# GpSimd takes two products of the mixing stage, its bursts lose their clears, and the denominator is scanned first

## The reference, cut to what matters

```python
x = x + attn_a(layernorm(x), ...)
x = x + ffn(layernorm(x), ...)       # 8 experts, 2 for each token
x = x + attn_b(layernorm(x), ...)    # mixing
x = x + ffn(layernorm(x), ...)
# mixing, for each batch and feature, over the 1024 tokens:
#   numerator aa and denominator bb are carried, pp is the running maximum
q = maximum(pp, u + kt);  e1 = exp(pp - q);  e2 = exp(u + kt - q)
y = (e1 * aa + e2 * vt) / (e1 * bb + e2)
q2 = maximum(pp + w, kt); e1 = exp(pp + w - q2); e2 = exp(kt - q2)
aa, bb, pp = e1 * aa + e2 * vt, e1 * bb + e2, q2
out = (sigmoid(r) * y) @ Wo.T
```

## Time and profile before

| | us |
|---|---|
| median of 3 runs | 1177.89 (1176.38 to 1179.65) |
| profiled execution, its own time | 1185.97 |
| its span | 1184.1 |
| busy over the span: PE, DVE, ACT, POOL | 842.3, 705.8, 571.2, 731.5 |
| POOL: row DMAs of `scatter`, 256 | 300.3 busy, 1173 ns each |
| POOL: clears, 508 | 133.2 busy, 262 ns each |
| POOL: idle until `place_i` | 203.6 |

### The profile page before, as it was taken

The page is one execution under the profiler, slowest core; times in us unless marked ns, Lnnn a source line. Parts: engine busy times, 40 slices in busy tenths (PEclk is TensorE's granted clock), DMA queues, the critical chain, the costliest instruction groups (busy, mean ns, idle before and its releaser), DMA issues.

```text
span 1184.1 us, 19270 instructions
## 1 busy us (share of the span) xinstructions
PE 842.3 (71%) x4480; PEld 667.6 (56%) x4481; DVE 705.8 (60%) x2510; ACT 571.2 (48%) x1588; POOL 731.5 (62%) x1127
## 2 busy tenths in 40 slices
PE   3787867767429889898755667566721988988981
PEld 1565656646318778787722334333420877877871
DVE  5697867845524444444647888889750343655555
ACT  3776646642213233333768887988620333323320
POOL 3017876736745777777710378787784576766774
PEclk9779878866659999999977888778755999999996
DMA  6022232112255555556412232231233555777874
GB/s 182 19 59 86 89 87 76 53 36 70 79 129 166 148 155 155 157 155 196 129 54 71 85 98 80 76 95 45 60 104 79 153 153 179 230 216 227 241 211 138
DMA packets 160255, 142.69 MB, mean 121 GB/s; under 512 B 17817, under 2 KB 133154, under 8 KB 160070
## 3 DMA queue, kind: packets, MB, share of 16 engines
q1 hardware_dynamic: 121744, 70.98, 21.9%
q10 hardware_dynamic: 20854, 37.24, 10.3%
q0 software_dynamic: 17600, 33.87, 8.4%
HBM read 93.47 MB, written 50.37 MB: 121 GB/s over the span
## 4 chain that ended last, share of the span: by engine, by line
PE 43%; ACT 17%; DVE 11%; issue 11%; POOL 7%; another core or an unknown queue 6%; DMA 2%; ACTq 2%; DVEq 1%; SPq 0%; POOLq 0%
PE banks L1055 16%; PE banks L1075 6%; POOL queue_dram L567 5%; PE banks L927 4%; PE banks L953 4%; ACT qkv L737 2%; ACT hmix L636 2%; PE banks L960 2%; PE banks L1110 2%; ACT gated L746 2%; PE banks L1063 2%; PE banks L1111 2%; PE banks L981 1%; DVE gated L1403 1%
## 5 line engine op out<-in xcount | busy, mean ns | idle before, releaser
L580 POOL DMA_INDIRECT result_dram<-ytile,result_row x284 | 277.9, 979 | 165.4 <-remote 57.5
L567 POOL DMA_INDIRECT queue_dram<-hffn,place_i x256 | 300.3, 1173 | 60.4 <-issue 46.0
L1055 PE MATMUL banks<-xt,tile_up 128*128 128x256 f32 x1136 | 286.2, 397 | 35.8 <-DVE gated L1403 31.6
L746 ACT ACTIVATE gated<-banks,tile_bias 128x256 f32<-128x256 f32 x284 | 119.2, 473 | 302.7 <-PE banks L1055 130.5
L1055 PEld LDWEIGHTS banks<-xt,tile_up 128*128 128x128 f32 x1136 | 213.4, 198 | 69.2 <-issue 28.3
L1403 DVE SCALAR_TENSOR_TENSOR gated<-banks,tile_bias,gated 128x256 f32<-128x256 f32 x284 | 124.2, 480 | 170.9 <-ACT gated L746 104.5
L1075 PE MATMUL banks<-wdown_sb,gated 128*128 x1136 | 156.4, 281 | 17.4 <-DVE ytile L1411 9.1
L1075 PEld LDWEIGHTS banks<-wdown_sb,gated 128*128 128x128 f32 x1136 | 142.0, 195 | 22.1 <-issue 21.7
L542 POOL MEMSET spacer<- 128x176 f32 x508 | 133.2, 262 | 0.4
L557 POOL COPY hffn<-top_f 128x4 f32<-128x4 f32 x32 | 5.0, 190 | 203.6 <-DVE place_i L1301 203.6
L1411 DVE TENSOR_TENSOR ytile<-banks,down_bias_sb 128x256 f32<-128x256 f32 x142 | 59.5, 419 | 76.1 <-remote 41.4
(11 more groups left out here) (203 smaller groups left out, 1570.2 us busy)
## 6 DMA issues: line engine op xcount, KB each, us to landing
tile_up<-w_up ACTq DMA_DIRECT2D x142, 256.0 KB
xtile<-queue_dram SPq DMA_DIRECT2D x142, 130.0 KB
qkv<-result_dram SPq DMA_DIRECT2D x24, 512.0 KB
x_dram<-xres SPq DMA_DIRECT2D x32, 256.0 KB
result_dram<-ytile,result_row POOLq DMA_INDIRECT x284
xin<-x SPq DMA_DIRECT2D x16, 256.0 KB
xold<-x SPq DMA_DIRECT2D x16, 256.0 KB
queue_dram<-hffn,place_i POOLq DMA_INDIRECT x256
```

The source lines that it names most:

```text
L567: nc.gpsimd.indirect_dma_start(queue_dram, bass.IndirectOffsetOnAxis(ap=place_i[s][:, at:at + 1], axis=0), hffn[s][c][:, j, :], None).then ...
L580: nc.gpsimd.indirect_dma_start(result_dram, bass.IndirectOffsetOnAxis(ap=result_row[i % SLOTS][:, h:h + 1], axis=0), ytile[i % SLOTS][:, h ...
L746: last = nc.scalar.activation(gated[i % GSLOTS][:, h, :], ps_up[i % 2][:, h, :], ACT.Silu, bias=tile_bias[i % STEP][:, h:h + 1])
L1055: last = nc.tensor.matmul(ps_up[i % 2][:, h, :], tile_up[i % WSLOTS][:, h * P:(h + 1) * P], xt[i % 2][:], start=True, stop=True)
```

## The change

- The bursts of the mixing stage (scatters 9 to 16) are issued without clears.
- VectorE's product of the denominator, `expo` part 0 times `den` into `y_den`, goes to GpSimd: `denominators(row)`. For rows 3 to 8 it stands amid the burst, behind the tenth DMA (`AMID = 9`); for rows 1 and 2, which have no burst beside them, by itself. It waits for VectorE's scan (`den_scanned`) and ScalarE's `now_ex`; VectorE waits for it (`den_scaled`) before its addition to `y_den`.
- VectorE scans the denominator first, then makes `ev`, then the shifts, then the numerator's scan.
- `weigh` of first halves goes from ScalarE (eight instructions) to GpSimd (one, 128 x 1024, the gates broadcast), behind the burst. ScalarE waits for both halves before the next clamps.
- The semaphore `numbered` and its wait in `scatter` go; `bias_in`, `split_out` and `rows_in` of the setup become one, `bias_moved`.

```diff
+            def denominators(row):
+                pool.wait_ge(den_scanned, row)
+                pool.sem_inc(place_taken, 1)
+                pool.wait_ge(now_ex, row)
+                pool.sem_inc(place_taken, 1)
+                nc.gpsimd.tensor_tensor(y_den, expo[:, 0, :], den[:, 0:SEQ], ALU.mult).then_inc(den_scaled, 1)
+            def weigh(m):
+                pool.wait_ge(gate_taken, m)
+                pool.sem_inc(place_taken, 1)
+                pool.wait_ge(results_in[0], m * 16)
+                pool.sem_inc(place_taken, 1)
+                nc.gpsimd.tensor_tensor(back_x[0], back_x[0], gate[:, 0:TPC * TOPK, None].to_broadcast([P, TPC * TOPK, D]),
+                                        ALU.mult).then_inc(weighted[0], 1)
...
                             nc.gpsimd.indirect_dma_start(
                                 queue_dram, bass.IndirectOffsetOnAxis(ap=place_i[s][:, at:at + 1], axis=0),
                                 hffn[s][c][:, j, :], None).then_inc(queued[s][c], 16)
+                            if row is not None and at == AMID:
+                                denominators(row)
                             if spread:
                                 space(at, BT * TOPK)
...
             experts(FIRST)
+            for b in (1, 2):
+                denominators(b)
+                weigh(b + 2)
             with pool.Fori(0, 2) as n:
-                scatter(n * 2 + (1 + BATCH), SECOND, 1, n + BATCH // 2)
-                scatter(n * 2 + (2 + BATCH), SECOND, 0, n + BATCH // 2)
+                scatter(n * 2 + (1 + BATCH), SECOND, 1, n + BATCH // 2, spread=False, row=n * 2 + 3)
+                weigh(n * 2 + 5)
+                scatter(n * 2 + (2 + BATCH), SECOND, 0, n + BATCH // 2, spread=False, row=n * 2 + 4)
+                weigh(n * 2 + 6)
             for b in range(BATCH - 3, BATCH + 1):
-                scatter(b + BATCH, SECOND, b % 2, (b + BATCH - 1) // 2, spread=b < BATCH)
+                scatter(b + BATCH, SECOND, b % 2, (b + BATCH - 1) // 2, spread=False, row=b + 2 if b + 2 <= BATCH else None)
...
                 if weighed:
                     take_gates(b + 2)
-                    weigh(0, b + 2)
...
                     weigh(1, b + 2)
-                    act.wait_ge(weighted[HALVES - 1], b + 2)
+                    for c in range(HALVES):
+                        act.wait_ge(weighted[c], b + 2)
...
             def states(row, between):
+                dve.wait_ge(past_ex, row)
+                nc.vector.tensor_tensor_scan(den[:, after], expo[:, 2, :], expo[:, 3, :], den[:, 0:1], ALU.mult, ALU.add).then_inc(den_scanned, 1)
+                weighted_values(row)
+                between()
                 dve.wait_ge(ev_ready, row)
-                num_done = mark(nc.vector.tensor_tensor_scan(num[:, after], expo[:, 2, :], ev, num[:, 0:1], ALU.mult, ALU.add))
-                between()
-                return num_done, mark(nc.vector.tensor_tensor_scan(den[:, after], expo[:, 2, :], expo[:, 3, :], den[:, 0:1], ALU.mult, ALU.add))
+                return mark(nc.vector.tensor_tensor_scan(num[:, after], expo[:, 2, :], ev, num[:, 0:1], ALU.mult, ALU.add))
...
-                need(den_done)
-                den_done = mark(nc.vector.tensor_tensor(y_den, expo[:, 0, :], den[:, before], ALU.mult))
                 need(num_done)
                 nc.vector.tensor_tensor(y_num, y_num, y_b, ALU.add)
-                need(den_done)
+                dve.wait_ge(den_scaled, row)
                 settle(nc.vector.tensor_tensor(y_den, y_den, expo[:, 1, :], ALU.add))
```

More of the change, by code:

```diff
@@ L275, in program @@
         consts_in, weights_in, rope_in, experts_in = sem("consts_in"), sem("weights_in"), sem("rope_in"), sem("experts_in")
-        bias_in, split_out, rows_in = sem("bias_in"), sem("split_out"), sem("rows_in")
+        bias_moved = sem("bias_moved")
         dve_step, act_step, place_step = sem("dve_step"), sem("act_step"), sem("place_step")
@@ L295, in program @@
             sem("seen_ready"), sem("count_ready"), sem("tail_ready"), sem("tails_queued"))
-        spaced, numbered, marked = sem("spaced"), sem("numbered"), sem("marked")
+        spaced, marked = sem("spaced"), sem("marked")
         started_ready, ends_ready, past_ready, entries_ready = sem("started_ready"), sem("ends_ready"), sem("past_ready"), sem("entries_ready")
@@ L311, in program @@
         clamped, den_ready, root_ready, inverted = sem("clamped"), sem("den_ready"), sem("root_ready"), sem("inverted")
-        ev_ready = sem("ev_ready")
+        ev_ready, den_scanned, den_scaled = sem("ev_ready"), sem("den_scanned"), sem("den_scaled")
         summed = sem2("summed")
@@ L327, in program @@
         PLACE_STEPS = 3
+        AMID = 9
         SCATTERS = 16 * TPC * TOPK
@@ L382, in _ @@
         def _(sp):
-            sp.dma_start(bias_sb[:], bias_cols).then_inc(bias_in, 16)
+            sp.dma_start(bias_sb[:], bias_cols).then_inc(bias_moved, 16)
             for c in range(HALVES):
@@ L544, in space, with scatter @@
                     clear.then_inc(spaced, 1)
-            def scatter(m, f, s, before, spread=True):
+            def denominators(row):
[11 more added lines that the diff above has]
+                                        ALU.mult).then_inc(weighted[0], 1)
+            def scatter(m, f, s, before, spread=True, row=None):
                 at = m * BT - (1 + f * BATCH) * BT
@@ L551, in scatter @@
                     pool.sem_inc(place_taken, 1)
-                    last = nc.gpsimd.tensor_copy(hffn[s][c][:, :, D], k_sb[:, bass.ds(at + (K_TOKEN + c * TPC), TPC)])
-                last.then_inc(numbered, 1)
+                    nc.gpsimd.tensor_copy(hffn[s][c][:, :, D], k_sb[:, bass.ds(at + (K_TOKEN + c * TPC), TPC)])
                 pool.wait_ge(place_ready, m)
@@ L558, in scatter @@
                 last.then_inc(marked, 1)
-                pool.wait_ge(numbered, m)
-                pool.sem_inc(place_taken, 1)
                 pool.wait_ge(marked, m + 1)
@@ L891, in _ @@
             act.wait_ge(split_done, 1)
-            nc.scalar.dma_start(split_dram.rearrange("i (p n) -> p i n", p=P), bias_parts[:]).then_inc(split_out, 16)
-            act.wait_ge(split_out, 16)
+            nc.scalar.dma_start(split_dram.rearrange("i (p n) -> p i n", p=P), bias_parts[:]).then_inc(bias_moved, 16)
+            act.wait_ge(bias_moved, 2 * 16)
             act.wait_ge(split_done, 2)
-            nc.scalar.dma_start(bias_rows[0:3, :], split_dram).then_inc(rows_in, 16)
+            nc.scalar.dma_start(bias_rows[0:3, :], split_dram).then_inc(bias_moved, 16)
             attention(None, None, 1)
@@ L1158, in _ @@
             pe.wait_ge(setup_done, 1)
-            pe.wait_ge(rows_in, 16)
+            pe.wait_ge(bias_moved, 3 * 16)
             project_qkv(1, range(BT))
@@ L1210, in settle @@
                 need(mark(ins))
-            dve.wait_ge(bias_in, 16)
+            dve.wait_ge(bias_moved, 16)
             settle(nc.vector.tensor_copy(bias_parts[:, 0, :], bias_sb[:]))
@@ L1552, in states, with outputs @@
             def states(row, between):
+                dve.wait_ge(past_ex, row)
+                nc.vector.tensor_tensor_scan(den[:, after], expo[:, 2, :], expo[:, 3, :], den[:, 0:1], ALU.mult, ALU.add).then_inc(den_scanned, 1)
+                weighted_values(row)
+                between()
                 dve.wait_ge(ev_ready, row)
-                num_done = mark(nc.vector.tensor_tensor_scan(num[:, after], expo[:, 2, :], ev, num[:, 0:1], ALU.mult, ALU.add))
-                between()
-                return num_done, mark(nc.vector.tensor_tensor_scan(den[:, after], expo[:, 2, :], expo[:, 3, :], den[:, 0:1], ALU.mult, ALU.add))
-            def outputs(row, num_done, den_done):
+                return mark(nc.vector.tensor_tensor_scan(num[:, after], expo[:, 2, :], ev, num[:, 0:1], ALU.mult, ALU.add))
+            def outputs(row, num_done):
                 dve.wait_ge(now_ex, row)
@@ L1584, in mixing @@
                 begin()
-                weighted_values(b)
                 def shifts():
@@ L1591, in shifts @@
                         scales_for_experts(b + (BATCH - 1))
-                scans = states(b, shifts)
-                outputs(b, *scans)
+                outputs(b, states(b, shifts))
                 if ahead:
```

## The result

| | before | after |
|---|---|---|
| median, us | 1178.1 (4 runs, 1176.38 to 1179.65) | 1200.26 (4 runs, 1191.99 to 1204.66) |
| ratio | | 1.018, interval 1.0119 to 1.0241 |
| span of the profiled execution | 1184.1 | 1202.8 |

A forecast was written before the change was run, and what follows sets the result against it. Only mixing was argued: VectorE, ScalarE and TensorE's ring, then GpSimd's bursts, set it; the change sends the ring through GpSimd. 10 + 2.1 + 2.7 - 0.5 = +14.3 us, so 1192 us, range 1172 to 1204.

The forecast's parts named there:

- Opening gap in every burst without clears: GpSimd's mixing bursts: idle time before the second DMA gives back 1.55 of the 2.0 us a burst that dropping clears saves.
- Products of 2.1 us: GpSimd's denominator product and weighing, 1024 columns: 2.1 us each, between a lower end of 1.03 and an upper of 2.9.
- Collisions ahead of the product: GpSimd's first ten row DMAs of a burst lose 3.2 of 4.6 us to VectorE's operations with two SBUF inputs.
- the clock of the batch: Time within one mixing batch, counted from zero at the placing of the batch before; next placing was at +32.6 us.
- The ring through GpSimd: Mixing, scatters 9 to 12: weighing ends +32.3, batch takes 35.5 us, four take 142 instead of 132.3, +10; chance 0.57.
- rival B: No change to tell: gap missing amid the rows, or cheap products; mixing ring 34.0 us a batch, +3, 1181 us; chance 0.13.
- The kernel before's ring: Mixing before the change: VectorE, ScalarE and TensorE set 32.6 us a batch, 132.3 us for four; GpSimd runs beside.
- Scatters 13 to 16: End of mixing: scatter 13 +2.1 from VectorE's lateness, last batch's placing +2.7, scatter 15 without clears -0.5 us.
- The sum: Whole kernel: 10 + 2.1 + 2.7 - 0.5 = +14.3 us, all from the mixing stage, giving 1192 us.
- Rival C: Slower still: in mixing VectorE and GpSimd hold each other up, `combine` 0.9 us later; +10, 1202 us; chance 0.12.
- second gap: In mixing bursts, the product amid the DMAs makes another opening gap, 1.55 us more a batch.
- Rival A: Faster: no opening gap, cheap products, mixing ring unchanged; needs gap and products under about 3.5 us; 1172 us; chance 0.18.

The follow-up runs named there:

- the weighing alone: Kernel before, clears kept, with only the weighing of first halves moved to GpSimd behind the bursts: 1164.91 us, ratio 1.0115.
- the last three kernels: Changed kernel, weighing back on ScalarE: product behind the sixth DMA, 1.0082; behind the fifth, 1.0026; back on VectorE, 0.9955 (ratios to kernel before).

## Why the forecast held, and where it did not

- **Opening gap in every burst without clears (1.55 us): wrong.** This is the step that failed. It comes in scatters 8 and 16, in every kernel looked at, and in no other, with or without clears. I had two bursts for it, which have something else in common: each is the last of its stage. Why that matters no row shows. It carried 6 us of the 14 (4 batches of 1.55).
- **Products of 2.1 us: nearly right.** 2.36 alone and 1.95 with the broadcast gates, 4.3 together where I had 4.2. (The lower end, redone from the two memsets, is 1.05 us and not 1.03; nothing hangs on it.) The Trainium skill (GPSIMD Engine Reference, 3.1 Elementwise — side-by-side cycle accounting) gave 2.25 by my estimate for the first; the rows are 5% above it.
- **Collisions ahead of the product, 3.2 us: a little low.** The three long DMAs of scatter 9 have 4.1 us over 0.97 each. The product came at 706.98, +18.0 on the clock of the batch, where I had +18.8: 1.55 earlier because the gap is missing and 0.3 because it follows the tenth DMA at once (706.96), and 0.9 later by the collisions. VectorE waited 4.56 us for it, where I had 4.7.
- **The ring through GpSimd: right up to the inversion, wrong behind the weighing, and mis-sized.** Factor done +22.9 (forecast +23.4), burst ends +29.1 (+29.9), weighing +31.0 (+32.3), `combine` +31.9 (+32.4), placing +34.7 (+35.5). Four batches take 136.3 or 136.4 us on all three chips where the changed kernel was profiled; I had 142. This is the 34.0 us a batch of rival B, the missing gap. But `combine` was not released by the weighing, as I had said it would be: it stands behind the cast that the weighing holds, and begins 0.85 us after the weighing's end, where I had 0.1 and the weighing alone shows 0.10. By an estimate from these rows the held cast is 0.75 us a batch, and 0.5 in scatter 12, 2.7 us in four.
- **The kernel before's ring** is not the same on each chip: 132.3 us on the first, 126.7 on the third. So the term, forecast +10, is +4.0 on the first chip and +9.7 on the third, with the same ring after.
- **Scatters 13 to 16: mis-sized.** Forecast +4.3, measured +1.4 on the first chip and +0.4 on the third. From 13 to 14 I had +2.1 (measured +0.6 and +1.4), from 14 to 15 +2.7 (+2.0 and +1.5), and from 15 to 16 -0.5 (-1.2 and -2.4): without the gap burst 15 gives back its clears.
- **The sum.** On the first chip mixing lost 5.5 us, nearer to rival B's 3 than to my 14; that the median still came out slower by more than the 14 was luck, owed to the attention and the first experts (+19.1) less the second experts (-5.9), which I had said are touched in nothing that costs. On the third and fourth chip the change costs 1.1%, which is 10 to 11 us, and on the third 10.0 of the 11.1 us of span lie in mixing. There the forecast of 1.2% is nearly met, because two errors cancel: the changed ring is 1.4 us a batch shorter than I had, and so is the ring of the kernel before on that chip.
- **Rival C** has its mechanism shown (VectorE held by GpSimd: 2.20 for 1.22, 2.94 for 0.73, 1.09 and 2.52 for 0.17), and a part of its price is in the changed kernel: with AMID 9 the product lies where VectorE stands and waits, but the cast under the weighing is held, about the 0.9 us a batch that C had for it. Its second gap never came.
- **Rival A** falls with the products' price: 4.3 us of the two together are over its 3.5, though the gap did not come, as it had said.

## What to carry to other kernels

Before work is taken from an engine, ask what the next thing it waits for is: VectorE's product stood ahead of a wait for TensorE, so its 1.13 us were worth nothing wherever GpSimd made it (VectorE had 1.67 to 2.26 us of idle time there in scatter 10 of the last three kernels). Work put on GpSimd is paid three times: in its own twice longer duration, in its place behind what is queued there, and in the small operations of VectorE that stand still beside it, which may be the ones on the chain. A cost read from two rows of a special place (here the last burst of each stage) is not the cost of the operation; ask what else is special about that place.

## What the runs showed of the hardware

- A GpSimd product of 128 x 1024 fp32 takes 2.36 us where VectorE is idle, 3.76 us begun over a scan on VectorE; four VectorE operations of 128 x 4 over it take 2.94 us instead of 0.73, and a cast of 128 x 16 takes 2.52 instead of 0.17. The cast was held though it began 0.57 us before the row of GpSimd's product, and four such shifts though they began 0.77 us before it.
- Indirect row DMAs of GpSimd follow each other every 1.27 us, 1.41 us with a clear of 176 columns between them; three of them beside VectorE took 2.0 to 2.7 us instead of 0.97.
- Between the first and the second row DMA lie 2.81 to 2.95 us in scatters 8 and 16 of all 14 profiles, and 1.27 to 1.49 in every other burst. The cause stays open.
- The same kernel takes 1178, 1155, 1081 and 1081 us on four chips at mean granted clocks of 0.83 to 0.84 in every profile. Part of the difference are idle times of ScalarE of 2 to 9 us with no known releaser, ahead of a copy whose input is there, in all six profiles of the first two chips and in none of the eight of the other two; part is in the second experts (298 us after scatter 16 against 258). The cause of either stays open.
